# Cross-attention on one core: q and k packed by plain transfers with permuted channels, and one reciprocal per tile over gathered denominators

## What is computed

```python
def reference(x, ctx, Wq, Wk, Wv, Wk_ip, Wv_ip, Wo, bo):      # x (2, 2048, 640), ctx (2, 77, 1024)
    text = ctx[:, :77, :]                                      # all of ctx; the "ip" part is empty
    q = split_heads(x @ Wq.T, 20)                              # 20 heads of 32 channels
    k = split_heads(text @ Wk.T, 20)
    v = split_heads(text @ Wv.T, 20)
    scores = einsum('bhsd,bhld->bhsl', q, k) / sqrt(32)
    out = merge_heads(einsum('bhsl,bhld->bhsd', softmax(scores), v))
    return out @ Wo.T + bo + x
```

## Time and profile before

| | |
|---|---|
| runs of the kernel before | 476.89, 473.17 and 476.56 us; median 476.56 |
| profiled execution, span from its first to its last instruction | 472.5 us |
| profiled execution, mean granted TensorE clock | 0.984 |
| busy: PE, DVE, ACT, POOL | 444.0, 390.6, 327.4, 230.9 us |
| busy share of the span: PE, DVE, ACT, POOL | 94, 83, 69, 49 % |

### The profile page before, as it was taken

The page is one execution under the profiler, slowest core; times in us unless marked ns, Lnnn a source line. Parts: engine busy times, 40 slices in busy tenths (PEclk is TensorE's granted clock), DMA queues, the critical chain, the costliest instruction groups (busy, mean ns, idle before and its releaser), DMA issues.

```text
span 472.5 us, 8672 instructions
## 1 busy us (share of the span) xinstructions
PE 444.0 (94%) x2538; PEld 316.6 (67%) x2538; DVE 390.6 (83%) x508; ACT 327.4 (69%) x633; POOL 230.9 (49%) x186
## 2 busy tenths in 40 slices
PE   8969988799899998999899998999899998999997
PEld 6857655467676766767576766676676766667765
DVE  0556998898989987898989889888989888898783
ACT  1759888867677784867678785868677775857620
POOL 5603685644547372544537373545446372532440
PEclk9999989999999998999999999999999998999999
DMA  8994422435344442444344453445344543334302
GB/s 282 397 229 139 113 74 74 114 90 163 96 123 131 121 154 77 149 113 146 100 131 132 122 154 113 112 121 172 97 121 118 143 126 91 90 91 140 107 24 111
DMA packets 37969, 61.44 MB, mean 130 GB/s; under 512 B 8241, under 2 KB 10033, under 8 KB 37937
## 3 DMA queue, kind: packets, MB, share of 16 engines
q1 hardware_dynamic: 27136, 41.36, 31.2%
q10 hardware_dynamic: 10800, 19.67, 13.1%
HBM read 28.81 MB, written 10.49 MB: 83 GB/s over the span
## 4 chain that ended last, share of the span: by engine, by line
PE 63%; DVE 18%; issue 6%; ACT 5%; SPq 3%; DMA 3%; ACTq 1%; DVEq 0%
PE ps_q L691 21%; PE ps_o L691 19%; DVE rden L566 7%; PE ps_s L739 7%; PE ps_pv L746 5%; PE ps_m L723 4%; DVE x_lo L534 4%; DVE mx L553 3%; PE ps_den L751 3%; ACT x_hi L368 2%; DMA x_f<-in_x 2%; DVE attn L575 1%; ACT p_f L421 1%; PE ps_m L790 1%; SPq L276 1%
## 5 line engine op out<-in xcount | busy, mean ns | idle before, releaser
L318 POOL TENSOR_TENSOR p_lo<-p_f,p_hi 77x512 f16<-77x512 f32 x120 | 146.7, 1229 | 180.3 <-ACT p_hi L425 180.3
L421 ACT ACTIVATE p_f<-ps_s 77x512 f32<-77x512 f32 x160 | 94.6, 591 | 58.9 <-PE ps_s L739 58.8
L566 DVE RECIPROCAL rden<-ps_den 128x256 f32<-128x256 f32 x80 | 134.7, 1720 | 0.4 <-PE ps_den L751 0.4
L425 ACT ACTIVATE p_hi<-ps_s 77x512 f16<-77x512 f32 x160 | 93.5, 584 | 2.0 <-PE ps_den L751 2.0
L553 DVE TENSOR_REDUCE mx<-ps_m 128x4 f32<-128x308 f32 x160 | 68.7, 471 | 21.8 <-PE ps_m L723 21.2
L691 PE MATMUL ps_q<-x_hi,wq_hi 128*128 128x512 f32 x200 | 80.7, 403 | 0.2
L691 PE MATMUL ps_q<-x_lo,wq_hi 128*128 128x512 f32 x200 | 79.6, 398 | 0.0
L691 PE MATMUL ps_q<-x_hi,wq_lo 128*128 128x512 f32 x200 | 79.5, 398 | 0.0
L403 ACT CAST q_packed<-q_hi 32x512 fp32r<-32x512 f32 x120 | 74.0, 617 | 2.4
L691 PE MATMUL ps_o<-attn_hi,wo_hi 128*128 128x512 f32 x170 | 70.9, 417 | 0.0
L691 PE MATMUL ps_o<-attn_hi,wo_lo 128*128 128x512 f32 x170 | 68.2, 401 | 0.0
(11 more groups left out here) (106 smaller groups left out, 614.1 us busy)
## 6 DMA issues: line engine op xcount, KB each, us to landing
x_f<-in_x SPq DMA_DIRECT2D x40, 256.0 KB, 3.2
q_packed<-q_hi SPq DMA_DIRECT2D x160, 64.0 KB, 2.1
q_packed<-q_lo SPq DMA_DIRECT2D x160, 64.0 KB, 2.0
x_res<-in_x ACTq DMA_DIRECT2D x35, 256.0 KB, 2.8
out<-out_sb ACTq DMA_DIRECT2D x35, 256.0 KB, 2.6
wk_sb<-in_wk SPq DMA_DIRECT2D x8, 320.0 KB, 5.8
wv_sb<-in_wv SPq DMA_DIRECT2D x5, 512.0 KB, 10.0
wq_sb<-in_wq SPq DMA_DIRECT2D x5, 320.0 KB, 9.1
```

Source lines behind the costliest of these rows:

```text
L318: nc.gpsimd.tensor_tensor(p_lo[:, i, :], p_f[:, i, :], p_hi[:, i, :], ALU.subtract).then_inc(plo_pool, 1)
L421: nc.scalar.activation(p_f[:, i, :], ps_s[i % 2][0:L, :], ACT.Exp, scale=SCALE).then_inc(pf_done, 1)
L425: nc.scalar.activation(p_hi[:, i, :], ps_s[i % 2][0:L, :], ACT.Exp, scale=SCALE).then_inc(phi_done, 1)
L566: nc.vector.reciprocal(rden[:, cols], ps_den[:, cols]).then_inc(rden_done, 1)
```

## The change

**Packing.** The rows of Wq and Wk are permuted on the host within each group of 128 (`heads_inside`), so that partition 4d + i of q and k holds channel d of head i. A transfer of 128 rows of q_hi into 32 rows with four heads side by side then keeps the order of its elements. The eight transfers of 64 KB and the four copies of `q_top` become three transfers of 256 KB for each unit, all from SP. k_packed has its axes swapped and is filled by three such transfers instead of four transfers, four ACT copies and four POOL copies. The block-diagonal k is made by ACT with a multiplication by a mask of heads (head_mask) over 128 partitions.

**Denominators.** The matrix of ones becomes six: for group g, ones[:, g, :] has ones only in the columns n of 32 with n mod 8 mod 5 equal to g. The groups of a tile add into one ps_den, and its row 32i + 8m + g then holds the denominator of head i of group g. DVE takes the reciprocal of ps_den once for each tile, in two halves, into rden_rows, in step (t, 0) of the next tile. SP then spreads 16 rows of it over 128 partitions, for each group by one transfer of 256 KB, into one of three slots of rden (`spread_rden`); groups 3 and 4 wait until the slots of groups 0 and 1 have been used. For each unit DVE copies ps_pv, times v's scale, into attn (`copy_values`) at the start of the next step, and multiplies attn by rden when that has landed (`normalise`). The last tile keeps the old way, with whole ones.

**Order.** The split of a finished attn is moved: ACT does chunk 0 ahead of `q_high` of step (t, 0), chunks 1 and 2 behind it, and 3 and 4 between the exponentials of step (t, 1); POOL and DVE follow. x_res also takes the finished output in place of out_sb, so that a residual is loaded only when the store of the slot's last user has landed.

```diff
+    def ends(t, g):
+        return g == 0 and exists(t) and exists(t - 1)
+    def ended(t, g):
+        return g == 1 and ends(t, 0)
+    def inverts(t, g):
+        return is_last(t) or (g == G - 1 and exists(t))
...
-        PACK = 16 * (2 * HG + 1)
+        PACK = 16 * (3 + 1)
...
-            sp.wait_ge(klo_done, G)
-            for i in range(HG):
-                sp.dma_start(k_packed[2 * D:3 * D, :, i, :].bitcast(F32),
-                             k_lo[D * i:D * (i + 1), :, :].bitcast(F32)).then_inc(kpack_in, 16)
+            for rows, src, done in (((0, D), k_hi, khi_done), ((2 * D,), k_lo, klo_done)):
+                sp.wait_ge(done, G)
+                for row in rows:
+                    sp.dma_start(k_packed[row:row + D, :, :, :].bitcast(F32),
+                                 src[:, :, :].bitcast(F32)).then_inc(kpack_in, 16)
...
+            def spread_rden(t):
+
+                sp.wait_ge(rden_done, 2 * (t + 1))
+                for c in range(G):
+                    if exists(slot_before(t, c)[0]):
+                        sp.wait_ge(norm_done, nth(*slot_before(t, c)) + 1)
+                    rows = rden_rows[c:P:DS, :].unsqueeze(1).to_broadcast([P // DS, DS, TB])
+                    sp.dma_start(rden[:, c % RS, :], rows).then_inc(rden_in[c % RS], 16)
+
             def pack_q(t, g):
-                for row, src, done in ((2 * D, q_hi, qhi_done), (D, q_lo, qlo_done)):
+                for rows, src, done in (((2 * D, 0), q_hi, qhi_done), ((D,), q_lo, qlo_done)):
                     sp.wait_ge(done, nth(t, g) + 1)
-                    for i in range(HG):
-                        sp.dma_start(q_packed[row:row + D, g % RS, i, :].bitcast(F32),
-                                     src[D * i:D * (i + 1), g % RS, :].bitcast(F32)).then_inc(pack_in[g % RS], 16)
+                    for row in rows:
+                        sp.dma_start(q_packed[row:row + D, g % RS, :, :].bitcast(F32),
+                                     src[:, g % RS, :].bitcast(F32)).then_inc(pack_in[g % RS], 16)
 
             def step(t, g):
                 if exists(shift(t, g, 1)[0]):
                     load_max(*shift(t, g, 1))
+                if ends(t, g):
+                    spread_rden(t - 1)
...
+                if ended(t, g):
+                    attn_low(t - 1, POOL_CHUNKS[1:])
...
+                if ends(t, g):
+                    attn_low(t - 1, POOL_CHUNKS[:1])
...
                 if exists(t):
                     exponentials(t, g, 0)
+                if ended(t, g):
+                    attn_high(t - 1, (3,))
+                if exists(t):
                     exponentials(t, g, 1)
+                if ended(t, g):
+                    attn_high(t - 1, (4,))
...
+                if ends(t, g):
+                    attn_high(t - 1, (0,))
                 if exists(shift(t, g, 2)[0]):
                     q_high(*shift(t, g, 2))
+                if ends(t, g):
+                    attn_high(t - 1, (1, 2))
...
+                nc.vector.tensor_scalar(attn[:, g, :], ps_pv[:, :], v_scale[:, g:g + 1], None,
+                                        ALU.mult).then_inc(pv_copied, 1)
...
+                dve.wait_ge(rden_in[g % RS], 16 * slot_uses(t, g))
+                nc.vector.tensor_tensor(attn[:, g, :], attn[:, g, :], rden[:, g % RS, :], ALU.mult).then_inc(norm_done, 1)
...
+                if exists(last_t) and not is_last(last_t):
+                    copy_values(last_t, last_g)
...
+                if ended(t, g):
+                    normalise(t - 1, 4)
+                    attn_low(t - 1, 3)
+                    q_low(*shift(t, 0, 2))
+                if inverts(last_t, last_g):
+                    invert_den(last_t, last_g, 0)
...
+                if ends(t, g):
+                    for c in range(4):
+                        normalise(t - 1, c)
+                    attn_low(t - 1, 1)
+                elif exists(shift(t, g, 2)[0]):
                     q_low(*shift(t, g, 2))
```

175 lines of the change are left out of this document (85 added, 90 removed).

## The result

The changed kernel took 521.56 us (median), the kernel before 476.56, which is 9.4% more. The ratio of 1.087 (95% interval 1.077 to 1.096) leaves out one disturbed execution of 847 us and two of 522 us, which lie over 1.5% above the fastest of the five (513.73). Timed again, in experiment 1, it took 522.1 us, ratio 1.096 (1.088 to 1.104). The forecast was 506 us, in a range of 484 to 525. The profile taken with the result is of the execution of 847 us, so all rows of after are of the profile of experiment 1, with a span of 521.0 us, 48.5 more than before.

A forecast was written before the change was run, and what follows sets the result against it. PE was taken as the bound, DVE costing only where late. Steps (t, 3) -4, first tile -5, start +3.5, six pairs +29 and the pair of t = 1 +6.4 gave +29.9 on 476.6: 506 us, range 484 to 525.

The forecast's parts named there:

- a chain with two trips: At each tile boundary: reciprocals spread by transfers, the fourth group's behind the first multiplication, landing at 10.65 and 14.0 us.
- the forecast's own case: Whole kernel: the likeliest outcome, 494 to 515 us, chance 0.55.
- steps (t, 3), six: Steps (t, 3), t = 1 to 6: wait for the product goes, copy of values partly replaces it, net -4 us.
- (0,2) to (0,4): First tile's steps without output tiles: waits for q_packed and PE's idle time go, -5 us, between 0 and -7.
- start, first values: Kernel start: more packing bytes queued ahead of the first row of maxima, +3.5 us, between 0 and 5.
- pairs t = 2 to 7: Steps (t, 0) and (t, 1): 25.35 us each, +29 us over six, including +1.0 for the last tile.
- pair t = 1: Steps (1,0) and (1,1): same chain after a short step without output tile, 25.35 against 18.97 us, +6.4.
- the schedule: Tile boundary timed by row durations from the values of (t, 0): PE transposes at 20.95 us, pair ends at 25.35.
- Rival 2: Tile boundary: trips cost nothing, DVE's order still does; pair 22.2 us, kernel 484; chance 0.2 for up to 492.
- The last tile: Last tile: half of its own reciprocal (1.7 us) precedes the reductions in place of the copy (0.7), +1.0 us.
- The bound by bytes: Kernel start: 1.06 MB more packing at 209 GB/s takes 5.1 us; +3.5 was taken.
- Rival 3, the clock: Seven tile boundaries: PE's waits bring its clock down, 1.5 us each, 10 us more, 517 us; chance 0.17.

The follow-up runs named there:

- experiment 1: The changed kernel run again with no edit: 522.1 us, ratio 1.096 to the kernel before.
- experiment 9: Changed kernel with the five multiplications reading a tensor that lies ready, so DVE's multiplications await no landing; all transfers and reciprocals stay: 496.84 us, ratio 1.045.
- experiment 4: Changed kernel with only groups 0 to 2 spread; groups 3 and 4 use the reciprocals of groups 0 and 1: 512.06 us, ratio 1.078.
- experiments 11 and 12: New packing with old denominators, cut by head: q in twelve transfers of 64 KB, 474.49 us (0.999); k in twelve of 96 KB, 468.96 us (0.983).
- the late loads: New packing with old denominators, five loads of Wq and Wv issued behind the first row of maxima: 468.74 us, ratio 0.986.

## Why the prediction was right, and where its sizes were off

Direction and mechanism were right: the boundary of tiles, where DVE gets a chain with two trips, sets the time, and little of the freed DVE and ACT time comes back (the 5.2 and 3.4 us of the first two rows). The size was not: +29.9 us were forecast, the medians differ by 45.0 and the spans by 48.5. The measured 521.56 lies in the range of 484 to 525, near its high end, and outside the 494 to 515 of the forecast's own case. Without the 3.2 us of (2,4) and (6,4), which no term had counted, it would lie at the very edge. Its terms, against the spans:

| term | forecast | measured |
|---|---|---|
| steps (t, 3), six | -4 (a step of 11.3) | -5.2 (11.15 to 11.21) |
| (0,2) to (0,4) | -5 | -3.4 |
| start, first values | +3.5 (first scores at 37 to 38) | +7.8 (first scores at 41.73; with the packing alone +6.3 and 39.54) |
| pairs t = 2 to 7 | +29 (25.35 each) | +43.4 (26.7 to 30.2) |
| pair t = 1 | +6.4 | +8.3 |
| (2,4), (6,4) at full clock | not counted | -3.2 |

**The waits were nearly all where they were named.** PE stands for DVE's attn_lo and for the maxima in (t, 1), and the values no longer wait in (t, 3). DVE stands 2.9 us in the mean ahead of the first multiplication. But its other stand, "2 us or so", was named ahead of the fourth, behind a second trip; there it is 0.3 us in the mean. In all seven tiles DVE stands ahead of the second, 0.9 us in the mean: the schedule let the first three transfers land together, and they land one behind the other. A further wait was not counted: in (t, 1) PE stands 0.6 to 1.0 us for q_hi ahead of the maxima (t = 2 to 7), where the schedule had 0.05.

**The pair.** The schedule's 25.35 us fell short by 2.1 for t = 2 to 6 (mean 27.5). As a cost the trips were sized right: the schedule gave them 1.9 + 1.25 = 3.15 us for a pair, and taking their waits away gave 27.5 - 24.5 = 3.0 (t = 2 to 6 of experiment 9, with the 0.4 of the clock), 0.8 of it the second (experiment 4). As durations they were not, and that the cost came out is in part luck: the first multiplication starts 3.5 us behind the reciprocal, where 2.6 was taken (no spread landed in under 3.0), and DVE stands 4.7 us for them; a part of that time is won back, it seems because without the stands DVE meets POOL more often. In (4,1) the fourth multiplication ends 16.0 us into the pair, where the schedule had 14.7: 0.85 by the first landing, the rest by the second landing and by the 1.71 us of the second multiplication.

The mis-sized term is the duration of DVE's two-input operations. Rival 2 said 22.2 for a pair without trips; it took 24.5. In (4,0) and (4,1) of experiment 9 the four multiplications took 4.24 us for the 2.8 of the schedule, attn_lo 1.80 for 0.85, p_lo 1.51 for 0.7: +3.2, less 1.1 for the other operations, which came a little closer together than assumed. The maxima were ready at 19.9 instead of 17.75. The prediction had the rule before it: the Trainium skill (SBUF — State Buffer, Who interferes with whom) says that a VectorE instruction with two SBUF inputs and a GpSimd instruction that reads SBUF contend, and that the second waits for the whole of the first. The rows of experiment 9 agree, with an end 0.54 us behind POOL's end in both cases read. The prediction put this into the width of its range, and took times near the undisturbed one for the sum, though the chain itself calls POOL's attn_lo exactly between DVE's operations, and though the trace before the change has a p_lo of DVE of 1.68 us in (2,1), where the schedule took 0.7 for the one in (t, 1).

**The last tile.** +1.0 was forecast over an ordinary pair; it took 30.17, 2.7 over the mean of the others. Here the fifth multiplication stood too, 1.21 us for its reciprocals, in the other tiles at most 0.3. Besides, (7,2) and (7,3) each grew by 0.7, since a half reciprocal stands ahead of the reductions in each unit of the last tile. The price of one, 1.7 against the copy's 0.7, was taken once and not for every step in which it stands.

**The start.** The bound by bytes, 5.1 us, was worked out and then lowered to 3.5, because of longer pieces and fewer issues. The packing alone brought the first scores 5.3 us later: the bound was right, the reduction was not, as experiments 11 and 12 show (with transfers cut by head the first scores come no earlier). In the nine profiles of kernels with this packing and early loads the first scores began between 39.5 and 41.7 us, the changed kernel's at the late end; where in this range a run lands stays open.

**Rival 3, the clock.** It was given 0.17 and came true in its premise: PE ran at half clock for 6.8 us at each boundary from t = 1 to 6 and twice for 3.4 us at t = 7, and the pairs of t = 2 to 7 had 0.87 to 0.89. Its price, 1.5 us for each drop on top, did not: with the clock at 1.00 the pairs kept all but 4.6 us. That its 517 us lie nearer to the measured time than 506 is chance. The drops here filled waits, and were hardly added to them.

**The packing.** The prediction counted its gain as -5 in tile 0 only, and its cost at the start. Alone it is 5 us faster than before, with 5.2 us gained in pairs that wait for DVE before the change. In the changed kernel this gain is swallowed: with the old packing it takes 517.03 us, with the new one 522.1 (the intervals of the two ratios overlap).

Three kernels are faster than both, all without the change of the denominators: the packing alone (ratio 0.992), with the late loads (0.986) and with k cut by head (0.983). Which of the three is the fastest the runs do not show. The denominators once for each tile are not worth having in this order of DVE's work.

## What to carry to other kernels

A reciprocal of 1.7 us beside a busy TensorE cost nothing here; one that was saved by gathering put its result, a trip through DMA and a row of multiplications on the one path that everything waited for at the end of a tile. Before moving work off a hidden engine, ask at which moment the new chain starts and who stands at its end. In such a chain, price VectorE's operations with two SBUF inputs by what GpSimd does at that moment, not by their minimum, and give transfers that are issued together a landing each. And where bytes through busy DMA engines delay the first work, price them at the rate of that stretch; a discount for larger transfers was wrong here.
